# Three 64-column products per block in the attention's value step, summed in the same PSUM columns

## The reference

```python
def xattn(query, key, value):              # 16 heads of 64; key = value = context
    # causal, in chunks of 512 keys with a running maximum: in effect
    scores = einsum('bhqd,bhkd->bhqk', q, k) * SCALE       # masked above the diagonal
    out = einsum('bhqk,bhkd->bhqd', softmax(scores), v)

x = x + xattn(layernorm(x), context, context)
weight = einsum('oin,n->oi', sigmoid(p) - sigmoid(n), exps * sigmoid(mask)) * scale
x = x + einsum('bsi,oi->bso', layernorm(x), weight) + bias
```

## Time and profile before

| | |
|---|---|
| runs, us | 1213.83, 1215.75, 1216.52 |
| the profiled execution, us | 1213.7 |
| its span, us | 1211.9 |
| mean granted clock | 0.982 |
| TensorE matmuls | 10788, busy 1109.8 us (92%) |
| TensorE weight loads | 10788, busy 803.6 us (66%) |
| VectorE | busy 968.1 us (80%) |
| ScalarE | busy 922.2 us (76%) |
| GpSimd | busy 687.4 us (57%) |

### The profile page before, as it was taken

The page is one execution under the profiler, slowest core; times in us unless marked ns, Lnnn a source line. Parts: engine busy times, 40 slices in busy tenths (PEclk is TensorE's granted clock), DMA queues, the critical chain, the costliest instruction groups (busy, mean ns, idle before and its releaser), DMA issues. The chain is left out here.

```text
span 1211.9 us, 28076 instructions
## 1 busy us (share of the span) xinstructions
PE 1109.8 (92%) x10788; PEld 803.6 (66%) x10788; DVE 968.1 (80%) x1424; ACT 922.2 (76%) x1898; POOL 687.4 (57%) x766
## 2 busy tenths in 40 slices
PE   4787889899999999889999999999999999899988
PEld 3676756566666776666766777676776676677753
DVE  5756677888888887888888887888888788888862
ACT  6899866688787787677787787788788787787750
POOL 3465546554446886454446986555348986463251
PEclk8889898999999999999999999999999999999999
DMA  9999726575759786675759886764658986654442
GB/s 317 287 321 330 256 71 118 129 148 108 150 121 175 178 186 130 140 141 106 151 120 201 150 191 128 159 158 107 127 119 199 183 173 143 135 105 97 86 88 70
DMA packets 382581, 190.88 MB, mean 158 GB/s; under 512 B 358128, under 2 KB 358128, under 8 KB 378352
## 3 DMA queue, kind: packets, MB, share of 16 engines
q1 hardware_dynamic: 381440, 189.05, 68.1%
q10 hardware_dynamic: 1008, 0.04, 0.1%
HBM read 67.15 MB, written 16.78 MB: 69 GB/s over the span
## 5 line engine op out<-in xcount | busy, mean ns | idle before, releaser
L533 ACT ACTIVATE p<-slot,mx 128x512 f32<-128x512 f32 (+7 forms) x512 | 378.0, 748 | 142.8 <-DVE mx L647 89.9
L647 DVE TENSOR_REDUCE mx<-slot 128x1 f32<-128x640 f32 (+7 forms) x352 | 356.8, 1016 | 32.4 <-PE slot L417 30.5
L464 PE MATMUL ffnb<-wt,yt 128*128 128x512 f16 x1464 | 373.0, 381 | 3.1 <-DVE ring L709 1.7
L653 DVE SCALAR_TENSOR_TENSOR pt<-ptb,pt 128x512 f16<-128x512 f32 (+1 forms) x504 | 281.9, 599 | 102.7 <-ACT pt L549 102.3
L413 PE MATMUL slot<-kt,qt 128*128 128x128 f16 (+3 forms) x1056 | 268.6, 284 | 16.4 <-ACT p L533 10.9
L414 PE MATMUL slot<-kt,qs 128*128 128x128 f16 (+3 forms) x1056 | 268.2, 284 | 0.0
L549 ACT ACTIVATE pt<-ptb 128x512 f16<-128x512 f32 (+1 forms) x504 | 239.9, 528 | 30.4 <-PE ptb L427 28.1
L427 PE MATMUL ptb<-id,p 128*128 128x128 f32 x1700 | 241.1, 280 | 12.2 <-DVE pt L653 10.4
L870 POOL TENSOR_TENSOR att<-osb 128x256 f32<-128x256 f32 x128 | 97.9, 765 | 271.0 <-ACT osb L556 266.4
L464 PEld LDWEIGHTS ffnb<-wt,yt 128*128 128x128 f16 x1464 | 136.9, 98 | 103.1 <-DVE ring L709 2.8
L446 PE MATMUL oacc<-v,pt 128*128 128x128 f16 x1700 | 180.3, 221 | 24.9 <-ACT osb L556 10.6
(11 more groups left out here) (90 smaller groups left out, 1451.1 us busy)
## 6 DMA issues: line engine op xcount, KB each, us to landing
ring<-in_x_dram SPq DMA_DIRECT2D x32, 512.0 KB, 4.3
cin<-in_ctx_dram SPq DMA_DIRECT2D x32, 512.0 KB, 4.6
out_dram<-ring SPq DMA_DIRECT2D x32, 512.0 KB, 3.4
qs<-qt SPq DMA_DIRECT2D x124, 128.0 KB, 2.9
v<-in_weights_dram SPq DMA_DIRECT2D x11, 1024.0 KB, 7.2
kt<-in_weights_dram SPq DMA_DIRECT2D x11, 1024.0 KB, 7.9
pd<-in_weights_dram SPq DMA_DIRECT2D x5, 1024.0 KB, 6.9
yt<-in_weights_dram SPq DMA_DIRECT2D x5, 1024.0 KB, 8.6
```

Source lines behind the costliest of these rows:

```text
L464: last = pe.matmul(dst, yt[:, k % 2, a * KT_N + kk, :], wt[:, c, kk, half * 512:half * 512 + 512], start=r == 0, stop=r == 3 * KT_N - 1)
L533: last = nc.scalar.activation(p32[:, j.par, hh * j.keys:(hh + 1) * j.keys], slot[:, j.par, base:base + j.keys], ACT.Exp, bias=mx[:, j.par, ...
L647: nc.vector.tensor_reduce(mx[:, j.par, 0:j.heads], src[:, 0:j.heads, 0:j.keys], AX_X, ALU.max, negate=True).then_inc(mx_ready, 1)
L653: nc.vector.scalar_tensor_tensor(pt[:, j.par, j.blocks + blocks.start:j.blocks + blocks.stop, :], ptb[:, c % 2, 0:P * len(blocks)].rearran ...
```

## The change

Each block's three products become three matmuls of 64 columns, all into the same 64 columns of PSUM, which TensorE adds up: p high with v high (L450), p high with v low (L451), p low with v high (L453). The first of them opens the accumulation and the third of the last block closes it. `oacc` is now a view of the first half of a bank called `obank`, 64 columns per head. ScalarE's copy of a group (L561) reads and writes 256 columns where it did 512, and `osb` is half as wide. GpSimd's addition of the halves (before L870) is gone, and with it the semaphore `osb_added`: the multiplication by the reciprocal (L875) reads `osb`, and ScalarE's copy waits for `att_ready` of the group two back, which that multiplication raises. The bias, which TensorE sums in the same bank twice near the start, keeps its 512 columns.

```diff
--- before.py
+++ after.py
@@ -195,7 +195,7 @@
         qs = sb("qs", [P, H, P], F16)
         p32 = sb("p32", [P, 2, 8 * P], F32)
         pt = sb("pt", [P, 2, 2 * 8, P], F16)
-        osb = sb("osb", [P, 2, GROUP, 2 * D], F32)
+        osb = sb("osb", [P, 2, GROUP, D], F32)
         att = sb("att", [P, GROUP, D], F32)
         y16 = sb("y16", [P, 2, KT_N, P], F16)
         yt = sb("yt", [P, 2, 2 * KT_N, P], F16)
@@ -244,8 +244,11 @@
 
         slot = stack.enter_context(nc.psum_tensor("slot", [P, 2, 1024], F32))
         ptb = stack.enter_context(nc.psum_tensor("ptb", [P, 2, 512], F32))
-        oacc = stack.enter_context(nc.psum_tensor("oacc", [P, GROUP, 2 * D], F32))
+        obank = stack.enter_context(nc.psum_tensor("obank", [P, 4, P], F32))
         ffnb = stack.enter_context(nc.psum_tensor("ffnb", [P, 512], F32))
+
+
+        oacc = obank[:, 0:2, :].rearrange("p a b -> p (a b)").rearrange("p (h d) -> p h d", d=D)
 
         first_kt = slot[:, 0, :].bitcast(F16).rearrange("p (h c) -> p h c", c=P)
         first_qt = slot[:, 1, :].bitcast(F16).rearrange("p (h c) -> p h c", c=P)
@@ -264,7 +267,7 @@
         s_done, mx_ready, p_done = sem("s_done"), sem("mx_ready"), sem("p_done")
         t_done, hi_done, lo_done, pv_done = sem("t_done"), sem("hi_done"), sem("lo_done"), sem("pv_done")
         p16_hi, p16_lo, pt_in = sem("p16_hi"), sem("p16_lo"), sem("pt_in")
-        osb_done, osb_added = sem("osb_done"), sem("osb_added")
+        osb_done = sem("osb_done")
         rinv_ready, att_ready, x1_ready = sem("rinv_ready"), sem("att_ready"), sem("x1_ready")
         q_stats, q_mv, q_rs, q_norm, q_hi, q_lo = (sem("q_" + n) for n in ("stats", "mv", "rs", "norm", "hi", "lo"))
         y_stats, y_mv, y_rs, y_norm, y_hi, y_lo = (sem("y_" + n) for n in ("stats", "mv", "rs", "norm", "hi", "lo"))
@@ -443,10 +446,12 @@
                     for blk in range(j.i + 1):
                         k = hh * (j.i + 1) + blk
                         v = v16[:, (j.t - j.i + blk) % V_PLACES, h]
-                        pe.matmul(oacc[:, h % GROUP, :], turned[:, k, :], v,
-                                  start=blk == 0, stop=False, skip_group_check=True)
-                        last = pe.matmul(oacc[:, h % GROUP, 0:D], turned[:, j.blocks + k, :], v[:, 0:D],
-                                         start=False, stop=blk == j.i, skip_group_check=True)
+                        dst = oacc[:, h % GROUP, :]
+                        pe.matmul(dst, turned[:, k, :], v[:, 0:D], start=blk == 0, stop=False, skip_group_check=True)
+                        pe.matmul(dst, turned[:, k, :], v[:, D:2 * D], start=False, stop=False,
+                                  skip_group_check=True)
+                        last = pe.matmul(dst, turned[:, j.blocks + k, :], v[:, 0:D], start=False, stop=blk == j.i,
+                                         skip_group_check=True)
                 last.then_inc(pv_done, 1)
 
             def linear(k, m0, m1, spare=None):
@@ -470,7 +475,7 @@
                 pe.wait_ge(bias_step, 18)
                 pe.wait_ge(osb_done, JOBS[BIAS_JOBS[r] - 2].group + 1)
                 for k in range(4):
-                    last = pe.matmul(oacc[:, k, :], ones32[:, :], bdiag[:, 4 * r + k, :], start=True, stop=True)
+                    last = pe.matmul(obank[:, k, :], ones32[:, :], bdiag[:, 4 * r + k, :], start=True, stop=True)
                 last.then_inc(bias_summed, 1)
 
             def weights(u):
@@ -552,8 +557,8 @@
 
             def output(g):
                 act.wait_ge(pv_done, LAST_OF_GROUP[g] + 1)
-                reached(act, osb_added, g - 1)
-                nc.scalar.activation(osb[:, g % 2], oacc[:, :, :], ACT.Copy, scale=1.0 / P_SCALE
+                reached(act, att_ready, g - 1)
+                nc.scalar.activation(osb[:, g % 2], oacc, ACT.Copy, scale=1.0 / P_SCALE
                                      ).then_inc(osb_done, 1)
 
             def q_split(t):
@@ -582,7 +587,7 @@
             def bias_part(r):
                 act.wait_ge(bias_summed, r + 1)
                 nc.scalar.copy(bias_row[:, :].rearrange("p (q j) -> p j q", j=8)[:, 4 * r:4 * r + 4, :],
-                               oacc[:, :, :]).then_inc(bias_out, 1)
+                               obank[:, :, :]).then_inc(bias_out, 1)
 
             def weights_high(u):
                 act.wait_ge(w_summed, 2 * u + 2)
@@ -866,11 +871,8 @@
             def add_attention(g):
                 pool.wait_ge(osb_done, g + 1)
                 reached(pool, x1_ready, g)
-                o = osb[:, g % 2]
-                nc.gpsimd.tensor_tensor(att[:, :, :], o[:, :, 0:D], o[:, :, D:2 * D], ALU.add).then_inc(osb_added, 1)
-                pool.wait_ge(osb_added, g + 1)
                 pool.wait_ge(rinv_ready, g + 1)
-                nc.gpsimd.tensor_tensor(att[:, :, :], att[:, :, :],
+                nc.gpsimd.tensor_tensor(att[:, :, :], osb[:, g % 2],
                                         rinv[:, g % 2, :].unsqueeze(2).to_broadcast([P, GROUP, D]),
                                         ALU.mult).then_inc(att_ready, 1)
                 pool.wait_ge(att_ready, g + 1)
```

## The result

| | before | changed |
|---|---|---|
| median, us (17 runs each) | 1213.83 | 1204.87 |
| lowest to highest, us | 1209.62 to 1218.88 | 1199.96 to 1212.03 |
| the profiled execution's span, us | 1211.9 | 1202.9 |
| mean granted clock | 0.982 | 0.984 |

The changed kernel takes 0.9928 of the time of before, with a 95% interval from 0.9915 to 0.9941: 0.72% or 8.7 us faster. Forecast was 1215.5 us, no change, with 1207 to 1232 us as range; the three runs known then had a median 1.9 us above that of all 17, which explains a small part of the miss and not the sign. Two executions on record in the experiments, one of 1280 us with y's split moved in the changed kernel and one of 2884 us of before, belong to the slow state and are in no ratio.

The account below looks back on a forecast made before the run. TensorE was taken to bound the kernel; +4.5 us (third matmul), -4.3 (copy) and -0.5 (GpSimd's addition) sum to -0.3 us, no change: 1215.5 us after adjusting to the runs' median, range 1207 to 1232 us.

Parts of the forecast that it names:

- What bounds the kernel: Whole kernel: TensorE bounds it, with occasional stalls for ScalarE, VectorE or a DMA; GpSimd's work counts almost nowhere.
- 78%: Value matmuls: share of their time on the critical path, 20.6 of 26.5 us in the last 120 us of attention.
- The third matmul: TensorE's value blocks: 85.0 to 87.5 ns each, +5.8 us over 2304 blocks, +4.5 us on the path.
- The weight loads: Rival, TensorE's value blocks: loads cannot start every 28 or 29 ns and set the spacing; 1251 or 1287 us, chance 0.13.
- The copy: ScalarE's copy out of PSUM: 599 to 380 ns, shortening TensorE's waits for it; -4.3 us.
- the upper bound: TensorE's waits for ScalarE's copy: 28 waits each give back 0.219 us, 6.1 us at most.
- the discount of 30%: TensorE's waits for ScalarE's copy: 70% of 6.1 us kept, the rest lost to later waits for VectorE or a DMA.
- a rival: The free-matmul rival, which said ScalarE's high parts behind the copy come sooner, shortening uncounted waits; 1209.2 us, chance 0.28.
- GpSimd's addition, -0.5 us: GpSimd: 97.9 us of removed work worth nothing itself; less blocking of VectorE's L661 gives -0.5 us.
- The bound of 4.4 us: VectorE's L661: most to be had from the removed addition, its 14% share of GpSimd's time applied to 31 us of waiting.
- Semaphores: ScalarE's copy: now waits for a multiplication two groups back instead of an addition; GpSimd is ahead, so zero.
- the free matmul: Rival, TensorE's value blocks: they stay at 85 ns and the copy's whole gain is kept; -6.6 us, 1209.2 us, chance 0.28.

Follow-up runs that it names:

- the narrow copy's case: Kernel before with ScalarE's copy reading 256 columns instead of 512, matmuls and GpSimd's addition kept, one product left out of the result: 0.9982, -2.2 us.
- the addition's case: Kernel before with GpSimd's addition removed, matmuls and ScalarE's copy kept, one product left out of the result: 0.9982, -2.2 us.
- fourth matmul: Changed kernel with a fourth 64-column matmul per block, written to columns nobody reads: 1.0237 of before, 37.5 us slower than the changed kernel.

## Why the prediction was wrong

**What bounds the kernel**: right in rank, too strong in degree. TensorE is first, but 56% of the 67 us added to it in the changed kernel reached the end, or some 64% without what L661 gave back, and not 78%. The 78% came from the last 120 us, and was applied to the whole span.

**The third matmul, +4.5 us**: right. A block went from 85.0 to 87.1 ns, where 87.5 were forecast from the 2.5 ns per matmul that 512 columns had shown as well, and the mean effect over the four settings is +4.6 us, or +4.9 with L661 taken out. The effect is between +1.3 and +10.2 us, according to the rest of the kernel, and 4.6 us of the 5.3 that a block's 2.3 ns make is 87%, not 78%; so the agreement of the mean is better than the method, and partly luck.

**The weight loads**: no effect; loads every 29 ns last, in runs of 32. The chance of 0.13 was spent on something that the rows could not exclude.

**The copy, -4.3 us**: right in mechanism, too small. TensorE's waits for it fell by 6.6 us, from 18.2 to 11.6 (the upper bound was 6.1), and in all four pairs of kernels with wide and narrow copy; the discount of 30%, for the next wait that takes over, was a guess, and the mean effect is -7.5 us, or -8.6 with L661 taken out. Beyond the waits, ScalarE's high parts behind the copy come sooner, which I had named in a rival and not counted: VectorE's waits for them fell by 9 to 14 us in all four pairs (102.3 to 93.3, 105.1 to 90.7, 106.1 to 93.1, 105.4 to 91.6 us). How much of that reached TensorE was not separated.

**GpSimd's addition, -0.5 us**: this is the step that failed. It is worth -7.0 us in the mean and -9.6 in the changed kernel. I read correctly that nobody waits for GpSimd in the chain and that VectorE's L661 can be blocked by it; but I sized that by the addition's share of GpSimd's busy time, "the neighbours that block are the 2 us ones", as if these stood still. They stand behind it in GpSimd's stream: 0.77 us less per group moves every long instruction against VectorE's stream. The bound of 4.4 us was too small for the same reason: it gave the addition its 14% of 31 us of waiting, while L661 fell by 10.7 us when the addition went from the otherwise changed kernel. Before's own 40 us of such waiting were not far from the 31.

**Semaphores, zero**: as forecast; ScalarE's copy waited for nobody but TensorE.

Of the rivals the free matmul was nearest in sign and time (1209.2 us), for a wrong reason. The change's sum by the mean effects is +4.6 - 7.5 - 7.0 = -9.9 us, and -8.7 was measured.

That the first of any two gains in before is worth only 2.2 us also follows L661. In the narrow copy's case it rose by 8.4 us. In the addition's case it fell by 2.5 us only: the waits behind y's split went from 20.5 to 12.4 us, but those behind the query's from 7.8 to 19.7. Before has L661 at 135.4 us where the other three kernels with an addition have 140.6 to 143.8. So the removal started from a kernel whose collisions were already fewer. Whether before's longer addition is what keeps them few stays open, and so do the 6 to 7 us that moving y's split gives in the changed kernel and not in before.

## What to carry to other kernels

An engine that no chain of waits names can still set the time, when its long instructions keep another engine out: ask not what the removed instruction blocks, but which long ones move when it goes, and what they then meet. The mark of it in a profile is a group whose mean is well above its shortest (here 1.47 us in the mean, and 1.62 us for the 1024 columns that also ran in 1.22), while its widths don't order its durations (768 columns took longer than 896). A change's parts tested one by one from the old kernel can each look small and still make the whole; all eight combinations of three parts were needed to see it, and even they had to be read beside the group that collides, since a part kept "in size" was not kept in time. The cure, three numbers in a table, was worth more than the change.

## What the runs showed of the hardware

A VectorE instruction with both inputs in SBUF that starts while GpSimd runs one of 2.1 us waits for that one's end: 2.73 us in place of 0.83 above. It holds throughout: in before 46 of L661's 92 start inside a GpSimd instruction of 1024 columns, and the 38 of them that lost more than 0.1 us all end at that instruction's end plus their own undisturbed time less 0.14 to 0.15 us. The Trainium skill's page "SBUF — State Buffer", section "Who interferes with whom", states that a VectorE instruction with two SBUF inputs contends with a GpSimd one that reads SBUF. The trace agrees. L653 and L647, which read at most one input from SBUF and the other from PSUM, keep their durations (598 and 1015 ns in the changed kernel, 599 and 1016 before); in before the 36 L653 of 512 columns that started inside a long GpSimd instruction took 686 ns, the 196 others 683.

Sixty-four-column matmuls, each with its own weight load, follow each other every 29 ns at the full clock, in runs of 24 (changed kernel) and of 32 (fourth matmul). Each costs about 2.5 ns above its columns (29.2 in place of 26.7 ns), as one of 512 columns does (215.8 in place of 213.3), and splitting 128 columns into two times 64 cost 2.1 to 2.5 ns.
